# A recurrence of 64 dependent steps: scatters behind the prediction, and four pieces of side work in other places

## The reference, cut to what matters

```python
z = sigmoid(x @ Wg.T + bg)
def step(h, inp):
    x_t, z_t = inp
    error = x_t - (h @ Wr.T + br)
    h_new = decay_factor * h + one_minus * (z_t * error)
    return (h_new, h_new)
_, ys = scan(step, 0, (x_t_first, z_t_first))        # 64 steps, one for each token place
y = layernorm(moveaxis(ys, 0, 1)) * ln_w + ln_b
return y @ Wo.T + bo
```

## Time and profile before

| what | us |
|---|---|
| median of 3 runs (lowest, highest) | 1359.72 (1355.3, 1359.99) |
| the profiled execution: its device time | 1357.04 |
| its span in the trace | 1355.3 |
| the first `predict` starts, after the span's start | 769.17 |
| the last one starts (step 63) | 941.22 |

### The profile page before, as it was taken

How to read it: one execution, slowest core, us unless ns; L and a number is a source line. 1 busy time by engine, 2 the same in 40 slices (tenths; PEclk the granted TensorE clock), 3 DMA queues, 4 the chain that set the end, 5 groups by cost and what they waited for, 6 DMA issues and landing times. The chain is left out here.

```text
span 1355.3 us, 29581 instructions
## 1 busy us (share of the span) xinstructions
PE 1232.2 (91%) x10417; PEld 733.4 (54%) x10418; DVE 730.2 (54%) x1573; ACT 337.1 (25%) x768; POOL 707.6 (52%) x762
## 2 busy tenths in 40 slices
PE   0899999999999999999989699999499999999994
PEld 0444434444443444443457456565378888888883
DVE  4555566555566655566259657777733323323325
ACT  2222233232233232233135211111311111111110
POOL 1055544345543445553139656787398553550872
PEclk9999999999999999999979899999599999999997
DMA  8645554434555444555054567863314443321556
GB/s 284 226 146 200 211 209 154 152 145 176 209 209 178 139 153 159 208 210 193 19 191 142 152 204 273 282 208 103 101 51 144 155 155 131 125 100 56 154 161 188
DMA packets 99376, 225.45 MB, mean 166 GB/s; under 512 B 14152, under 2 KB 30664, under 8 KB 95216
## 3 DMA queue, kind: packets, MB, share of 16 engines
q1 hardware_dynamic: 87872, 189.46, 40.9%
q0 software_dynamic: 10288, 33.57, 7.4%
q10 hardware_dynamic: 1152, 1.57, 0.4%
HBM read 179.21 MB, written 45.35 MB: 166 GB/s over the span
## 5 line engine op out<-in xcount | busy, mean ns | idle before, releaser
L326 POOL TENSOR_TENSOR wb<-w,hcb 128x512 f32<-128x512 f32 x120 | 122.1, 1038 | 315.2 <-DVE hcb L683 292.9
L401 PE MATMUL S<-ctxT,x 32*64 32x416 f32 (+1 forms) x4096 | 185.2, 511 | 15.9 <-DVE ctxT L627 15.9
L401 PEld LDWEIGHTS S<-ctxT,x 32*64 32x64 f32 x4096 | 108.5, 133 | 94.8 <-issue 45.8
L329 POOL TENSOR_TENSOR wb<-wb,w 128x512 f32<-128x512 f32 x120 | 150.0, 1271 | 0.0
L609 DVE STREAM_TRANSPOSE ctxT<-ctx_one 128x1024 f32<-128x1024 f32 (+1 forms) x128 | 115.1, 949 | 13.5 <-DMA ctx_one<-in_ctx_dram 13.2
L436 PE MATMUL O<-ctx_one,probsT 128*64 128x512 f32 (+1 forms) x448 | 110.4, 608 | 0.0
L1929 POOL TENSOR_TENSOR w_low<-w_low,w_high 128x2048 fp32r<-128x2048 f32 x21 | 96.7, 4607 | 1.7
L522 ACT ACTIVATE x<-S,w2R,w3R 128x128 f32<-128x128 f32 x256 | 92.7, 472 | 19.5 <-PE S L392 19.5
L2114 DVE TENSOR_TENSOR f_hL<-f_TH,f_hH 128x512 fp32r<-128x512 f32 x39 | 27.0, 692 | 120.4 <-ACT f_hH L2067 117.3
L634 DVE TENSOR_REDUCE mx<-S 128x1 f32<-128x832 f32 x16 | 16.4, 1025 | 128.1 <-PE S L401 128.1
L1452 PE MATMUL Pb<-WrT,yT 128*32 128x128 f32 x2016 | 69.8, 280 | 13.7 <-DVE yT L1705 13.1
(11 more groups left out here) (286 smaller groups left out, 2497.6 us busy)
## 6 DMA issues: line engine op xcount, KB each, us to landing
ctx_one<-in_ctx_dram SPq DMA_DIRECT2D x64, 512.0 KB, 4.5
x<-in_ctx_dram SPq DMA_DIRECT2D x16, 1536.0 KB
ctx_two<-in_ctx_dram SPq DMA_DIRECT2D x16, 1536.0 KB, 9.4
ctx_one<-in_ctx_dram SPq DMA_DIRECT2D x64, 256.0 KB, 5.5
w_low<-_L_ffn_gate_up_proj_dram POOLq DMA_DIRECT2D x10, 1024.0 KB, 8.1
f_xt<-routed_x SPq DMA_DIRECT2D x39, 256.0 KB
routed_y<-f_yt SPq DMA_DIRECT2D x39, 256.0 KB
w_low<-_L_ffn_gate_up_proj_dram SPq DMA_DIRECT2D x6, 1024.0 KB, 8.0
```

The costliest lines, as they stand in the source:

```text
L326: pool.tensor_tensor(wb[:, slot, b], w3[:, c], hcb[:, c, b, None].to_broadcast([P, D]), ALU.mult).then_inc(wb_step, 1)
L329: pool.tensor_tensor(wb[:, slot, b], wb[:, slot, b], w0[:, c], ALU.add).then_inc(wb_ready, 1)
L401: last = pe.matmul(S[64 * b:64 * b + 64, a, 0:tiles * Q], qr[a * Q:(a + 1) * Q, k, 64 * b:64 * b + 64], ctxT[a * Q:(a + 1) * Q, 0:tiles, b ...
```

## The change

It has five edits, all in `recurrence`:

1. POOL: half 1 of `add_bo` goes from step 3 to step 1, ahead of the scatter. In body 1 the halves stand in steps 2 and 3 instead of 0 and 3.
2. POOL: each scatter of a body with steps waits until `pred_full` has the value of its own step.
3. PE: `logits` is cut in two. Chunks 0 and 1 stay in step 2, chunks 2 and 3 go to step 3, ahead of `prefix`.
4. PE: `turn_weight(3)` and `bo_product(3)` go from the end of body 0 to behind the first `predict` of body 1; the `Wo` products of tile 0 move back by one step, with two quarters in step 3; `turn_router` goes to step 1. `turn_y` of tile 0 waits for three turned blocks.
5. DVE: `add_lnb` goes from ahead of step 1 of body 1 to behind it.

```diff
+                    half = st - 2 if k == 1 else st
+                    if 0 <= half < 2 and has(k - 1):
+                        add_bo(k - 1, 1 - s, half, bo_loads)
                     if st == 2 and has(k - 1):
                         power2(k - 1, 1 - s)
                     if st == 3 and has(k - 2):
                         power3(k - 2)
                     if st in (1, 2) and has(k - 5):
+                        pool.wait_ge(pred_full, ST * k + st)
                         scatter(k - 5, (n - 5) % RING, st - 1)
-                    if st in (0, 3) and has(k - 1):
-                        add_bo(k - 1, 1 - s, st // 3, bo_loads)
...
-            def logits(j):
...
+            def logits(j, chunks):
+                if 0 in chunks:
+                    pe.wait_ge(xn3T_ready, j + 1)
...
+                for c in chunks:
                     last = pe.matmul(Lg[:, 0:B], xn3T[:, c, :], gwT[:, c, None, :].to_broadcast([P, B // E, E]),
                                      start=(c == 0), stop=(c == C - 1))
-                last.then_inc(lg_done, 1)
+                if C - 1 in chunks:
+                    last.then_inc(lg_done, 1)
...
             def turn_y(j, s):
+                if first(j):
+                    pe.wait_ge(wo_ready, C - 1)
...
-                    if first(k) and st >= 2:
-                        turn_weight(st)
-                        bo_product(st)
-                    if k1(k) and st == 0:
+                    if first(k) and st == 2 or k1(k) and st == 0:
+                        turn_weight(2 if first(k) else 3)
+                        bo_product(2 if first(k) else 3)
+                    if k1(k) and st == 1:
                         turn_router()
...
-                        wo_chunk(k - 1, 1 - s, st)
+                        for c in ((), (0,), (1,), (2, 3))[st] if k1(k) else (st,):
+                            wo_chunk(k - 1, 1 - s, c)
...
-                    if st == 2 and has(k - 3):
-                        logits(k - 3)
+                    if has(k - 3) and scan and st >= 2:
+                        logits(k - 3, (2 * st - 4, 2 * st - 3))
+                    if has(k - 3) and not scan and st == 2:
+                        logits(k - 3, range(C))
...
-                if k1(k):
-                    add_lnb()
                 if has(k - 2):
                     residual(k - 2, s)
...
                     scan_step(k, s, 1, loads)
                 if first(k):
                     scale_wo(2)
+                if k1(k):
+                    add_lnb()
```

More of the change, by code:

```diff
@@ L1454, in predict @@
                 last.then_inc(pred_full, 1)
-            def logits(j):
[L1457 to L1462, removed]
+            def logits(j, chunks):
+                if 0 in chunks:
+                    pe.wait_ge(xn3T_ready, j + 1)
+                    if first(j):
+                        pe.wait_ge(gwT_ready, 1)
+                    if has(j - 1):
+                        pe.wait_ge(ex_ready, j)
+                for c in chunks:
                     last = pe.matmul(Lg[:, 0:B], xn3T[:, c, :], gwT[:, c, None, :].to_broadcast([P, B // E, E]),
                                      start=(c == 0), stop=(c == C - 1))
-                last.then_inc(lg_done, 1)
+                if C - 1 in chunks:
+                    last.then_inc(lg_done, 1)
             def wo_chunk(j, s, c):
```

## The result

| | before | after |
|---|---|---|
| median of 7 runs (lowest, highest), same chip, us | 1355.79 (1353.98, 1359.99) | 1350.01 (1346.48, 1352.31) |
| profiled execution, us | 1357.04 | 1346.48 |
| last `predict` starts, after the span's start | 941.22 | 930.25 |

The ratio is 0.9942, 95% interval [0.9926, 0.9958]: by the interval the change saves 5.7 to 10.0 us, and the two medians are 5.8 apart, where 2.1 were forecast. The sign was right and the size was not. It went the way of rival A, PE's pace. The seven-run median of before is 3.9 under the three-run median on which the forecast was put, so only the difference is to be compared.

The account below looks back on a forecast made before the run. It took the one-step chain from prediction through `m`, `H` and turn, with PE work, scatter stalls and load waits, as the bound. Start -2.0, late bodies -1.0, loaded bodies +0.9, logits 0: -2.1 on 1359.72, 1357.6 us; range 1349 to 1365.

Parts of the forecast that it names:

- rival A: Late bodies: compares slip between POOL operations, every late body takes 10.07 us; -9.1 in all, 1350.6 us; chance 0.25.
- What bounds the kernel: Recurrence steps: one-step chain with a 2.17 us floor; a scatter lies over the 0.82 us stall in six steps 1.
- the -0.82 of edit 2: Step 1 of stalled bodies: scatters that wait remove the stall, at best falling to PE's 2.51 us, -0.82 each.
- Half 1 in step 1, half 0 over `row_places` (edit 1): Late bodies: adds lengthen DVE operations; `m` at 1.8, step 1 at 2.80 us; step 0 +0.35 us.
- Loaded bodies: Bodies 6, 7 and 9: half 1 lengthens POOL's chain after the load, +0.3 us each, +0.9 in the sum.
- Logits in halves: Late bodies: step 2 falls to 2.42 us, step 3 rises to 2.63; sum 0, between -0.3 and +0.3.
- The start: Body 1: earlier first and second predictions, body 2 at 787.7 to 788.4 against 790.16; -2.0 us, between -2.6 and -1.0.
- B: Late step 1: the stall moves, a later scatter holds `m` back to 3.1; +5.9 us, 1365.6; chance 0.15.
- C: Bodies 3 to 9: load queue gives the gain back, longer POOL chain costs more; +1.8 us, 1361.5; chance 0.1.
- D: Late bodies: the stall isn't the scatter's, `m` stays at 2.3, step 0 loses; +0.4 us, 1360.1; chance 0.08.

Follow-up runs that it names:

- w_only: Old kernel with only the scatters' wait for their own step's prediction added; median 1352.12 us, ratio 0.9986.
- x_wait: Changed kernel with half 1 of `add_bo` back in step 3 beyond body 1 and expert weight loads behind the next `xt` load; median 1344.10 us, ratio 0.9913.
- after_nowait: Changed kernel without the scatters' wait for the prediction; median 1348.85 us, ratio 0.9948 to the old kernel.
- after_again: Changed kernel with no further edit, traced a second time; median 1350.43 us, ratio 0.9958 to the old kernel.
- x_first: Changed kernel with each 1 MB expert weight load behind the next `xt` load in SP's queue; median 1342.03 us, ratio 0.9886 to the old kernel.
- lg_start: Old kernel with halved logits and the PE and DVE start changes, without moved half 1 or scatter wait; median 1352.45 us, ratio 0.9967.
- best: lg_start with each expert weight load behind the next `xt` load; median 1348.86 us, ratio 0.9945 to the old kernel.
- probe_act: Old kernel plus a small ACT copy waiting for the same `pred_full` value as `m` of step 1, bodies 5 to 15; one run, 1363.17 us.
- lg_only: Old kernel with only `logits` cut in halves; median 1350.47 us, ratio 0.9970.
- start_only: Old kernel with only the PE and DVE start changes, body 1's two adds in steps 2 and 3; median 1351.02 us, ratio 0.9972.

## Why the prediction was right or wrong

**What bounds the kernel.** Right. The stall of steps 33, 45, 49, 53, 57 and 61 went with the scatter, and it was pure loss: without it the step falls to PE's pace, 2.50 in step 1 of body 13 in `w_only` and `x_wait`, the -0.82 of edit 2. Its share of the waiting was read too high (6.1 of 29.6 us).

**Half 1 in step 1, half 0 over `row_places` (edit 1). This step failed.** The contention in step 1 was foreseen with nearly the right length (0.77 for the compare, 0.70 in the earlier trace rows), but its price was reckoned on DVE and not against PE. In step 0 I added 0.35 to 2.51. The half lies there, but `m` is at 1.30 where before has 1.22, and PE's own 2.50 covers up to 0.25 more. In step 1 I put `m` at 1.8 and the step at 2.80; `m` came at 1.58 and the step took 2.59. So edit 1 costs 0.09 per late body instead of 0.64, five times over: 2.75 of the 4.0 us by which the late bodies beat the forecast. The rest is spread: before takes 11.12 and 11.07 in bodies 11 and 12, where I had put 10.89 for each, and the halves of `logits` give 0.08 in each. It was rival A that had this right (10.07 for a body, 10.06 measured), and its row was there: PE with 10.24 of 11.00 busy.

**Loaded bodies.** The chain is as forecast: from the add to `H` of step 3 are 7.59 in body 7 (849.26 - 841.67), where I had 7.6. That is 0.63 more than the 6.96 of before, so the longer chain is real, but no +0.9 comes of it: bodies 2 to 10 are 0.9 to 2.7 shorter. Part of this is the stall that before has in 7.1 or 8.1. It is not that the loads are waited for less (13.4 against 13.0). How much each edit takes in these bodies stays open, since the same kernel differs there by 1.8 from trace to trace.

**Logits in halves.** Right: 2.43 and 2.54 where 2.42 and 2.63 were forecast. The sum of the two steps is 0.08 less than in before. Its worth beside the shift is small.

**The start.** Right in kind, 1.2 too small. The first prediction of body 1 came at 776.56 (forecast 776.7), the second at 779.26 (779.6 to 780.3), body 2 at 786.84 (787.7 to 788.4). Before has a granted clock of 0.58 from 778 to 782, with the prediction of 1.93 in the earlier trace rows; after has 1.00 from 776 to 780, and its `turn_weight` takes 0.66 instead of 1.11. I had counted the lower clock for one prediction and not for what stands around it. The double quarter of `Wo` in step 3 cost less, 2.92 instead of 3.3.

**Rivals.** B fell: a scatter from 906.50 to 907.56 doesn't hold `m` back, for `pred_full` has already come. C fell: the start's gain is still there at body 11. D fell. A was right about the late bodies, and I gave it 0.25 because I held the lengthened compare against it without asking what covers it. That its 1350.6 is so near the measured 1350.01 is luck: A took off 9.1 from 1359.72, and measured are 5.8 off 1355.79.

**Time.** The traces give 9.0 to 10.9 us and the medians 5.8. The profiled executions of after are 3.0 and 3.5 under their medians. The ten runs of `after_nowait` lie up to 9.5 apart, the four or five of each kernel with the turned load order 0.5 to 2.6. So the spread seems to go with the load waits, though the runs are few. Why the profiled executions fall on its better side is open.

## What to carry to other kernels

When an edit makes an operation of one engine slower, hold the new start of its result against the time at which the next engine is free, before a price is put on it: here `m` could come 1.49 behind its prediction instead of 1.15 in a step of 2.50, free of charge (step 1 of body 12 of after). In a step whose next engine is not busy that long, the lengthening would count. A chain of short steps should be looked at for asynchronous work that lies over the signal that it waits for. Here it was enough to move it behind that signal, by an operation ahead of it or by a wait. In a queue that feeds a chain, small loads with a due time go ahead of large ones without: 8.4 us by the medians between `after_again` and `x_first`, 3.6 between `lg_start` and `best`. And when single edits are set against the old kernel, the old kernel should be traced on the same chip: two kernels whose edits seemed to cure the stall had been traced where it may not occur.

## What the hardware showed

A scatter in flight over the end of a group of matmuls can make the semaphore of that group late: in before `m` starts 2.31 instead of 1.15 behind the group's start, and in `probe_act` ACT and DVE are late alike. In the 43 steps of six traces that have it, and in 14 milder ones of five others, `m` starts 1.4 to 1.6 behind the start of the scatter. A scatter that has ended by 0.44 behind the group's start does nothing (909.50 plus 1.06 in after, against the prediction at 910.12). The ten steps of `lg_only` and `start_only` have a scatter in flight there and no delay, all of them on chip 3. Whether it is the chip, and what holds the semaphore up, no run shows.

A wait of 4.7 us for a load cost not only itself. TensorE, busy for 0.45 of the 3.00 us ahead, was at the 1.2 GHz level (granted clock 0.50) for the next 3 us, and the next step took 1.63 more (4.51 against 2.88).
